# Half of ScalarE's transpose copies in the attention phase moved to VectorE

## The reference

```
xn = layernorm(x)
q = xn @ Wq.T + bq ; k = ... ; v = ...
q = q * t + rotate_every_two(q) * t      # t: table of sines and cosines; k likewise
scores = q @ k.T / sqrt(512)
probs  = softmax(scores)
attn   = probs @ v
h   = layernorm(xn) * gamma + beta
h   = gelu(act_quant(h) @ weight_quant(w1).T / scales + b1)
ffn = act_quant(h) @ weight_quant(w2).T / scales + b2
out = x + attn + ffn
```

## Time and profile before

| what | us |
|---|---|
| median of 2 runs | 2963.88 (2943.05 and 2984.7) |
| the profiled execution | 2944.43 |
| its span on the slowest core (core 4) | 2942.9 |
| spans of the eight cores | 2922.2 to 2942.9 |
| phase B on that core, by the timeline | about 655 to 1706 |

### The profile page before, as it was taken

The page is one execution under the profiler, slowest core; times in us unless marked ns, Lnnn a source line. Parts: engine busy times, 40 slices in busy tenths (PEclk is TensorE's granted clock), DMA queues, the critical chain, the costliest instruction groups (busy, mean ns, idle before and its releaser), DMA issues. The chain is left out here.

```text
span 2942.9 us, 32116 instructions; the slowest of 8 cores (2922.2 to 2942.9 us)
## 1 busy us (share of the span) xinstructions
PE 1796.4 (61%) x7504; PEld 708.3 (24%) x7652; DVE 1383.4 (47%) x2220; ACT 1056.4 (36%) x2813; POOL 144.0 (5%) x265
## 2 busy tenths in 40 slices
PE   0088888867655555676777712565556666666666
PEld 0033333322222222222222301222222222222222
DVE  2344444432232322444444305666666666666664
ACT  0033333324444344444454503333333333333332
POOL 0000000000000000111111102000000000000000
PEclk9988888878887888888898866777777777777778
DMA  3211111112222222433444271000000000000000
GB/s 101 89 51 54 54 55 53 45 51 63 92 80 70 83 83 76 147 104 111 133 143 133 79 250 37 22 22 22 22 22 22 22 22 22 22 22 22 22 15 15
DMA packets 53102, 187.88 MB, mean 64 GB/s; under 512 B 7467, under 2 KB 7599, under 8 KB 51894
## 3 DMA queue, kind: packets, MB, share of 16 engines
q0 software_dynamic: 29280, 100.73, 10.4%
q1 hardware_dynamic: 23638, 85.08, 9.0%
HBM read 152.17 MB, written 33.55 MB: 63 GB/s over the span
## 5 line engine op out<-in xcount | busy, mean ns | idle before, releaser
L957 PE MATMUL ps<-big,xqfm 128*128 128x512 bf16 x1000 | 272.3, 419 | 96.7 <-ACTq L180 96.2
L671 PE MATMUL ps<-big,qfm 128*128 128x512 bf16 x1004 | 249.9, 407 | 115.6 <-ACTq L180 101.7
L723 PE MATMUL ps<-big,pT 128*128 128x512 bf16 x992 | 264.5, 407 | 48.4 <-ACTq L180 46.3
L339 PE MATMUL psT<-identb,nhq 128*128 128x128 bf16 x512 | 95.2, 241 | 313.5 <-DVEq L180 263.4
L349 ACT COPY hqfm<-psT 128x128 bf16<-128x128 bf16 x512 | 136.3, 266 | 384.8 <-PE psT L339 340.7
L1019 PE MATMUL ps<-big,hqfm 128*128 128x512 bf16 x992 | 261.1, 421 | 3.0 <-issue 1.8
L714 ACT COPY pT<-psT 128x128 bf16<-128x128 bf16 x512 | 136.3, 266 | 141.4 <-PE psT L708 83.7
L465 PE MATMUL ps<-wk_mix,xnfmA 128*128 128x512 bf16 x481 | 163.6, 499 | 6.8 <-ACTq L180 5.7
L671 PEld LDWEIGHTS ps<-big,qfm 128*128 128x128 bf16 x1024 | 103.7, 103 | 254.8 <-issue 150.9
L339 PE MATMUL psT<-identb,xnA 128*128 128x128 bf16 x256 | 55.3, 250 | 174.6 <-ACTq L180 160.6
L957 PEld LDWEIGHTS ps<-big,xqfm 128*128 128x128 bf16 x1024 | 96.5, 104 | 235.5 <-issue 159.9
(11 more groups left out here) (151 smaller groups left out, 2565.7 us busy)
## 6 DMA issues: line engine op xcount, KB each, us to landing
wch<-w1T POOLq DMA_DIRECT2D x64, 512.0 KB, 4.7
wch<-w2T POOLq DMA_DIRECT2D x64, 512.0 KB, 4.3
xinA<-x_full SPq DMA_DIRECT2D x32, 512.0 KB, 3.6
schi<-sck_hi SPq DMA_DIRECT2D x32, 256.0 KB, 2.6
xinB<-x_own SPq DMA_DIRECT2D x16, 512.0 KB, 4.7
partial<-outB POOLq DMA_DIRECT2D x16, 512.0 KB, 6.2
w1q_sp<-wst POOLq DMA_DIRECT2D x32, 256.0 KB, 2.4
w2q_sp<-wst POOLq DMA_DIRECT2D x32, 256.0 KB, 2.5
```

The source lines that it names most:

```text
L339: t_op(lambda e, bi=bi, sc=sc: e.transpose(psT[bi][:, 0:128], src[:, sc:sc + 128], identb[:]), [stok, "identb"], [f"psT{bi}"], f"{tag}.T{j}")
L671: t_op(lambda e, ej=ej, kc=kc, bk_i=bk_i, qf=qf: e.matmul(ps_[bk_i][:], qf[:, ej * 128:(ej + 1) * 128], big0[:, ej * S + kc * 512:ej * S + ...
L723: e.matmul(ps_[bk2][:], pT[sub][:], big1[:, kt64 * H + half * 512: kt64 * H + half * 512 + 512], start=first, stop=(kt64 == 31)),
L957: t_op(lambda e, dj=dj, hc=hc, bk_i=bk_i: e.matmul(ps_[bk_i][:], xqfm[:, dj * 128:(dj + 1) * 128], big0[:, dj * FF + hc * 512:dj * FF + hc ...
```

## The change

Three groups of copies out of the `psT` banks, all in phase B, are shared between the two engines: pieces 1, 3, 5 and 7 of `xnfmB` and of `qfm` (by the argument `ev_alt`, which `emit_tr` has already), and pieces 1 and 3 of each block's `pT`. The data, the buffers and the order on PE stay. The lines behind L714 move down by six: L730 becomes L736, L735 becomes L741, the copies of `pT` are L715 (ScalarE) and L720 (VectorE).

```diff
                 def stage1_pe(qt):
                     emit_tr(xnB, "xnB", 8, xnfmB, "xnfmB", lambda j: j * 128,
-                            f"B{qt}.xn", per_chunk=True)
+                            f"B{qt}.xn", per_chunk=True, ev_alt=True)
...
                     emit_tr(qro, "qro", 8, qf, qftok, lambda j: j * 128,
-                            f"B{qt}.q", per_chunk=True)
+                            f"B{qt}.q", per_chunk=True, ev_alt=True)
...
-                            s_op(lambda e, sub=sub: e.copy(
-                                    pT[sub][:], psT[sub][:, 0:128]),
-                                 [f"psT{sub}"], [f"pT{sub}"],
-                                 f"B{qt}.pE{kc}.{sub}")
+                            if sub % 2 == 0:
+                                s_op(lambda e, sub=sub: e.copy(
+                                        pT[sub][:], psT[sub][:, 0:128]),
+                                     [f"psT{sub}"], [f"pT{sub}"],
+                                     f"B{qt}.pE{kc}.{sub}")
+                            else:
+                                v_op(lambda e, sub=sub: e.tensor_copy(
+                                        pT[sub][:], psT[sub][:, 0:128]),
+                                     [f"psT{sub}"], [f"pT{sub}"],
+                                     f"B{qt}.pE{kc}.{sub}")
```

## The result

The changed kernel took 3004.57 us (median of 11 runs), the kernel before 2951.39 us (median of 10, beside it); the ratio is 1.0171, 95% interval 1.0140 to 1.0202. The ratio is that of the undisturbed runs alone: in four of the eleven (3037 to 3057 us) the cores of one die or of both ran at a lower clock, so the two medians would give 1.0180. The profiled execution took 3008.57 us, its spans 2984.1 to 3007.0 us. The prediction was 3007.0.

The account below looks back on a forecast made before the run. Phase B was taken as a chain of waits with no engine full, VectorE's chain setting the quantising tiles. The terms summed to +62.6 us on the profiled 2944.4, giving 3007.0; range 2990 to 3025, chance 0.48.

Parts of the forecast that it names:

- points 1 and 2: Sharing pT copies gains 2.6 us a tile in tiles 0-6 and 15; sharing qfm gains 1.1 where ScalarE's exp is next.
- point 3: Six projections beside abs work: xnfmB copies wait behind VectorE's last abs chunk, qro transposes at +8.3 instead of +2.0, +6.3 us.
- point 4: Places without point 3's loss: tile 3 -4.5 us (xnfmB -0.8), tile 7's projection -0.8, first projection -1.9, tile 15 -2.6.
- point 5: Tiles 7 to 14: copies ahead of quantisation on VectorE delay its chain, +6.3 and +0.8 us a tile, +56.8 in all.
- 6.6 us to the first L567: Tiles 7 to 14: first quantisation instruction 6.6 us behind the qro transposes instead of 0.30, summed from 2.7, 2.57, 1.15, 0.19.
- 0.8 for chunk 1: Tiles 7 to 14: after block 0's slow matmuls chunk 1 waits for PE, its load chain moving by about 0.8 us.
- One sign that I named: Prediction wrong if PE still waits for VectorE ahead of the third score chunk; that wait was 2.94 us behind tile 10.
- Rival 1: Quantising tiles: a thinned-out chain gets wch loads 0.7 us sooner, giving back 24 us in all; 2983 us, chance 0.20.
- Rival 2: Tiles 7 to 14: PE stays at the 1.2 GHz level, blocks take 4.9 us, +20 us; 3027 us, chance 0.18.
- Rival 3: ScalarE binds every tile, all 16 gain 2.6 + 1.1 us, points 3 and 5 cost nothing; -59, 2885 us, chance 0.07.
- rival 4: Whole change: gains of points 1 and 2 and the losses cancel, so nothing changes; 2944 us, chance 0.07.

Follow-up runs that it names:

- e5: Kernel before with pieces 1 and 3 of pT copied on VectorE only outside tiles 7 to 14 (tiles 0 to 6 and 15); ratio 0.9942.
- e6: Kernel before with only the qfm copies shared between ScalarE and VectorE; ratio 1.0039.
- e4: Kernel before with only the xnfmB copies shared between ScalarE and VectorE; ratio 1.0126.
- e1: Kernel before with pieces 1 and 3 of pT on VectorE in tiles 7 to 14 alone; ratio 1.0213.
- e2: Kernel before with pieces 1 and 3 of pT on VectorE only in block 0 of tiles 7 to 14; ratio 1.0196.
- e12: Changed kernel plus the next chunk's load recorded ahead of the store and two store buffers; ratio to the kernel before 1.0111.
- e7: Kernel before with pT shared outside tiles 7 to 14, qfm for tiles 0 to 7, xnfmB for tiles 0, 4, 8; ratio 0.9903.
- e8: Changed kernel with the xnfmB copies back on ScalarE; ratio to the kernel before 1.0059.
- e3: Kernel before with pieces 1 and 3 of pT on VectorE only in blocks 4 to 7 of tiles 7 to 14; ratio 1.0084.
- e10: e7 plus the next chunk's load recorded ahead of the store and two store buffers in turn; 2897.36 us, ratio to the kernel before 0.9807.

## Why the prediction was right

The steps against the traces, mean over the eight cores, in us:

| step of the prediction | predicted | measured |
|---|---|---|
| points 1 and 2, half of tiles 0 to 6 | 7 x -3.7 = -25.9 | 7 x -3.6 = -25.4 |
| point 3, projections beside abs work | 6 x +6.3 = +37.8 | 5 x +6.5, and +4.6 in tile 0: +37.0 |
| point 4, xnfmB in the scores of tiles 3 and 7 | 2 x -0.8 = -1.6 | 2 x -1.4 = -2.7 |
| point 4, first projection | -1.9 | -1.3 |
| point 4, tile 15 | -2.6 | -2.7 |
| point 5, tiles 7 to 14 | 8 x +7.1 = +56.8 | 8 x +6.6 = +52.6, and +1.1 in the scores of 8-14 |
| sum | +62.6 | +58.6 |

In this execution cores 2 and 3 were slowed by their clock (last section). On the six others the first row is 7 x -4.0, the projections are 5 x +6.3 and +4.6, the scores of tiles 3 and 7 2 x -1.7, tiles 7 to 14 8 x +6.6, and tile 15's outB comes 54.7 us later.

*Points 1 and 2* were right in mechanism and size, each by itself too (e5 2.7 for 2.6, e6 1.3 for 1.1).

*Point 3* was right: the wait moved to the fifth xnB transpose, the qro transposes came at +8.3, and e4 shows the loss alone.

*Point 5* was right in mechanism (e1, e2, e12) and 8% too large. Its 6.6 us to the first L567 were 6.13: L694 came at 2.24 instead of 2.7, the other terms (2.57, 1.15, 0.19) measured 2.56, 1.13 and 0.20. Its 0.8 for chunk 1 did not come: the third L567 starts 8.05 us behind the first, in the kernel before 7.80, and in the mean over all tiles and cores 8.4 in both. The second starts 1.4 us later than it did (4.10 instead of 2.69 behind the first), and the wait for the load behind it, 1.63 us in the earlier trace rows, covered that. What the sum did not have is 0.5 us between the eighth L567 and the write of outB (3.8 instead of 3.3); its cause was not looked for.

*The sum against the metric.* The profiled executions differ by 64.1 us (3008.57 and 2944.43), the medians by 53.2. Some 10 us of the 64.1 are the clock of four cores in that one execution (last section): the longest span of a core without it is 2996.9, 54.0 above the longest before, and at tile 15 the six cores without it in phase B are 54.7 us late. So the change costs 53 to 55 us, the sum had 62.6, and the ratio, 1.7% (at most 2.0% by its interval), lies below the 2.1% that the sum gives. On those six cores point 5 was 4 us too dear and point 3 2 us; points 1 and 2 gained 2 us more than predicted, and so did the scores of tiles 3 and 7. That 3007.0 met 3004.57 so closely is luck in part: the sum was some 8 us too large, and the execution it was added to, 2944.4, lay 7 us below the median of its kernel.

*One sign that I named was wrong.* I wrote that I would be wrong if PE still waited for VectorE ahead of the third score chunk. It does (core 4, behind tile 10):

```profile
1445.04 8.79 PE L671 MATMUL ps<-big,qfm 128*128 128x512 bf16 x39 [1.99 <-DVEq L180]
```

The wait shrank from 2.94 to 1.99: PE itself is now held by VectorE's copies block by block (the rows at 1489.49 and 1502.63), and both arrive late. It said nothing about the theory.

*The rivals.* Rival 1 (loads absorb part): the eight chunks kept their pace (28.5 and 29.7 us in tile 11), nothing was given back. Rival 2 (clock) came true for single pieces and not at its price: the granted clock from tile 7 to 8 is 0.87 against 0.89 before, six matmuls take 1.46 us right behind a wait of 1.08, but 2.72 behind one of 2.25 (the row at 1502.63). Beyond the first block 4.2 matmuls a tile run at the 1.2 GHz level in tiles 7 to 14 (0.2 before), in 54 of the 64 tiles of the eight cores three or more. They did not slow the chunks, which follow each other in 4.3 us and not in this rival's 4.9. Rival 3 (faster) and rival 4 (nothing) fall with the result. Rival 3 would have been right for a part: with copies only where VectorE has nothing waiting behind them (e7) the kernel is 1.0% faster. The rule of the Trainium skill that I had set beside it (Perfetto Trace Analysis, Identifying the Most-Contended Engine: optimize the engine of highest occupancy first), applied to ScalarE and VectorE, pointed the wrong way here; relieving ScalarE, 29.4 us busy in 61 against VectorE's 28.0, cost 6.6 us a tile.

## What to carry to other kernels

A copy moved to an engine that has waits to fill costs little by its duration and may cost much by its place: look at what stands behind it in that engine's order, and at what it has to wait for itself. Ahead of a chain that transfers pace it costs the whole delay of its own producer once per chain (here 6 us for two copies of 0.23 us), and busy time saved elsewhere does not pay for that. Where a chain waits for a load, look for the second limit right behind it (here the single store buffer) before expecting anything from the first.

## What the hardware showed unexpectedly

In the profiled execution of the changed kernel, cores 2 and 3 ran the blocks of tiles 1, 2, 4 and 5 in 2.85 us instead of 2.47. Core 3, tile 2:

```profile
856.93 2.26 PE L729 MATMUL ps<-big,pT 128*128 128x512 bf16 x8 [0.26 <-ACTq L180]
859.02 0.44 PE L708 MATMUL psT<-identb,probs 128*128 128x128 bf16 x4
859.78 2.26 PE L729 MATMUL ps<-big,pT 128*128 128x512 bf16 x8 [0.33 <-ACTq L180]
```

Eight matmuls take 2.26 us, between the 1.89 of the other tiles and the 3.57 at 1.2 GHz. The granted clock of that stretch (852 to 876) is 0.75; over the whole half it is 0.70 to 0.74 in these four tiles and 0.87 in tiles 0, 3 and 6. It costs these cores about 10 us in these halves, most of what their qro transposes of tile 7 (1218 and 1219 us) came behind the other cores' (1199 to 1205).

Cores 0 and 1, the other two of that die, have none of it in phase B, and have it in phase C, in stretches between 2420 and 2805 us. Core 0, sixteen matmuls of one line before and within:

```profile
2197.81 3.61 PE L1025 MATMUL ps<-big,hqfm 128*128 128x512 bf16 x16
...
2485.01 4.37 PE L1025 MATMUL ps<-big,hqfm 128*128 128x512 bf16 x16
```

From tile 15's outB to its end core 0 took 1253.5 us, 11 more than in the kernel before (1242.4); cores 4 to 7 took 1239.8 to 1243.1. So the two longest spans, 3007.0 of core 3 and 3006.4 of core 0, both carry some 10 us of it.

It belongs to single executions, not to the order of the work. In e12, with the same program in tiles 0 to 6, all eight cores show blocks of 2.47, and so do e5, e7 and e8. In e3, whose tiles 0 to 6 are those of the kernel before, cores 6 and 7 have it in tiles 0, 1, 3 and 4, and cores 4 and 5 in phase C; in e10 cores 6 and 7 have it in tiles 0 and 1. Core 7 of e3, tile 0:

```profile
707.27 2.26 PE L729 MATMUL ps<-big,pT 128*128 128x512 bf16 x8 [0.33 <-ACTq L180]
...
710.18 2.26 PE L729 MATMUL ps<-big,pT 128*128 128x512 bf16 x8 [0.33 <-ACTq L180]
```

The matmuls take as long, yet the block takes its old 2.91 us, because ScalarE sets the pace there. This is a cost of the change that no point of the prediction has: where PE sets the pace, a lower clock lengthens the block.

The cause of the level stays open. The Trainium skill (TensorE: Matmul & The Clock Gate, Part 1) tells of a limiter that takes a whole die to 13/16 of the full clock. The 1.89 and 2.26 us, a ratio of 0.84, are near that; that two cores of a die had it where the two others had not is not what the page states.
